# A graph layer with routed experts: three parts instead of two, two rows of a chunk normalized on GpSimd, and other numbers in the table that sets the order

## The chip, the cores and the metric

The kernel runs on one core of one Trainium2 chip. The metric is device time in microseconds for one execution. Three runs of the kernel before took 1494.88, 1497.17 and 1503.07 us, so the median is 1497.17 us. The profiled execution is a fourth one; it took 1489.54 us.

## The reference, cut to what matters

There are 6250 nodes with 256 features and 106250 edges sorted by destination. All numbers are float32.

```
xn = layernorm(x)
agg = segment_sum(xn[src] * edge_weight, dst);  gnn = agg @ weight
q, k, v = split(xn @ Wqkv.T) in 8 heads of 64;  k, v normalized per head
mix = (q @ (k^T v) / n) @ Wout.T + bout          # k^T v sums over all nodes
x2 = x + gnn + mix
y = layernorm(x2)
top 2 of 16 experts by y @ gate_w + gate_b, softmax over the two
moe = sum over the two of (relu(y @ w1[e] + b1[e]) @ w2[e] + b2[e])
out = x2 + layernorm(y + moe) * gamma + beta
```

## The kernel before

**Rows and batches.** The nodes are 49 row tiles of 128. The edges are 70 batches of up to 12 gathers; one gather (GpSimd, line 873) fetches 128 normalized rows from DRAM by source. There are 831 gathers. TensorE sums a batch with 12 small products (line 1528, called edges below), places the sum in its window of nodes (line 1537), and VectorE adds it (line 1132). The ring of gathered rows holds two batches, so the gathers of batch b wait until the edges of batch b-2 are done (`after(pool, batch_done, b - 1)` ahead of line 873).

**Opening.** The rows of x come in 7 chunks of 7 tiles. VectorE takes statistics (line 1020), ScalarE the root (line 885), VectorE the reciprocal (line 1029); then ScalarE normalizes 5 tiles of the chunk (line 889) and VectorE 2 (line 1035). SyncE writes each chunk to the table in DRAM (line 713). The first gather waits for the whole table and for a flag (line 1081) that says the edge tables have the expected form.

**Work beside the gathers.** On TensorE, between the edges of one batch and the next, stand: `kv` of each row tile (keys, values and their sum), one `mid` (the weights folded together), `mix` of a group of two row tiles (attention and graph output), `gate` of a group (VectorE and ScalarE: normalize, choose two experts), `rank`, `slots`, `line`, `list` of a stretch of row tiles (places of its rows in lists by expert; only rank and list have products on TensorE, lines 1637 and 1645; slots is some 9 us of small VectorE instructions, lines 1283 to 1356). GpSimd then scatters the stretch's rows to their slots (line 843, two per row tile), and expert tiles of 128 slots can run (`moe`: a transposition at line 1652, first layer 1664, second layer 1677, and the sum with the bias on VectorE, line 1461).

**Parts.** `PT` cuts the 49 row tiles into parts. An expert's rows fill tiles of 128 slots, and within a part a tile is shared by stretches; at the end of a part each expert's last tile is closed, however full. `SUB` cuts the parts into stretches. The reference's own routing, counted with the inputs of the run, gives 89 tiles in part 0 (row tiles 0 to 39) and 28 in part 1 (40 to 48). When all tiles of a part are done, GpSimd picks up its results (line 856, two per row tile) and VectorE finishes the rows (`fin1`, `fin2`, lines 1479 to 1509) and SyncE stores them. Picks use the ring, so they start only after the last batch.

**The order.** `plan()` walks the batches with a table of prices in us (`EDGES_PE`, `KV_PE`, `TAKEN_PE` for an expert tile, `LANDS` and others) and writes down which pieces stand after the edges of which batch, and where in GpSimd's stream scatters and picks stand. Every engine follows that list in order; nothing is chosen at run time but whether a possible tile exists. What stands after the last batch is the tail.

Of the kernel before, what the change touches and what calls it, by code (L numbers as in the profile page):

```python
# [8 lines left out]
ALU = mybir.AluOpType  # L9
# [7 lines left out]
CH = 7  # L17
NC = 7
NT = NC * CH
# [19 lines left out]
NW = NP // GW  # L39
ACT_ROWS = 5  # L40

E, F = 16, 512
# [9 lines left out]

PT = (0, 40, NT)
SUB = (0, 8, 16, 24, 32, 36, 40, NT)
NPART, NSUB = len(PT) - 1, len(SUB) - 1
# [79 lines left out]
GATHER, SCATTER = 1.254, 1.28  # L135
EDGES_PE, KV_PE, MID_PE, MIX_PE, GATE_PE, TAKEN_PE, LEFT_PE = 2.4, 5.0, 18.0, 2.3, 0.01, 3.9, 0.5
RANK_PE, LAG, SPARE, LANDS = 0.7, 6.0, 4.0, 4.0

# [219 lines left out]
def gps_layer(nc, x, src, dst, first_dst, edge_w, gnn_w, wkv, wq, wout, bout, gate_w, gate_b,  # L358
# [5 lines left out]
    with ExitStack() as ctx:  # L364
# [3 lines left out]
        def sem(name):  # L368
            return ctx.enter_context(nc.semaphore(name))
# [4 lines left out]
        X2 = sb("X2", [P, NT, D])  # L374
# [151 lines left out]
        dve_consts = sem("dve_consts")  # L526
        tables_in = sem("tables_in")
        later_in = sem("later_in")
        x_in = sems("x_in", NC + 1)
# [3 lines left out]
        normed = sem("normed")  # L533
        dve_normed = sem("dve_normed")
        table_out = sem("table_out")
# [144 lines left out]
        TABLES = [(dstrel[:, :].bitcast(I32), dst), (first_i, first_dst.to_broadcast([P, NG]))]  # L680
        CONSTS = [(ew[:, :], edge_w), (src_sb[:, :], src), (wkv_sb, wkv)]
        LATER = [(wq_sb, wq), (wout_sb, wout), (gnn_sb[:, :, 0:D], gnn_w), (gate_sb[:, :, :], gate_w),
# [10 lines left out]
        def rows_of(t, q, n=1):  # L693
            return t[q * P:(q + n) * P, :].rearrange("(j p) d -> p j d", p=P)
# [6 lines left out]
        def _(sp):  # L701
# [8 lines left out]
            for c in range(NC):  # L710
                sp.wait_ge(normed, ACT_ROWS * (c + 1))
                sp.wait_ge(dve_normed, c + 1)
                sp.dma_start(rows_of(table, c * CH, CH), X2[:, c * CH:(c + 1) * CH, :]).then_inc(table_out, 16)
            for o, i in LATER:
                sp.dma_start(o, i).then_inc(later_in, 16)
# [79 lines left out]
        def _(pool):  # L795
# [18 lines left out]
            for s, t in dealt.items():  # L814
# [4 lines left out]
                          allow_small_or_imprecise_dtypes=True).then_inc(pool_consts, 1)  # L819

            pool.wait_ge(table_out, 16 * NC)
            pool.wait_ge(flag_ready, 1)
# [58 lines left out]
        def _(act):  # L881
            act.wait_ge(pool_consts, 2)
            for c in range(NC):
                act.wait_ge(stats_done, c + 1)
                act.activation(std0[:, c * CH:(c + 1) * CH], mv[:, c * CH:(c + 1) * CH, 1], ACT.Sqrt,
                               bias=eps_t[:]).then_inc(std_done, 1)
                act.wait_ge(rstd_done, c + 1)
                for q in range(c * CH, c * CH + ACT_ROWS):
                    act.activation(X2[:, q, :], X2[:, q, :], ACT.Identity, bias=nmr[:, q:q + 1],
                                   scale=rstd[:, q:q + 1]).then_inc(normed, 1)  # L890
# [122 lines left out]
        def _(dve):  # L1013
# [12 lines left out]
            def scale_chunk(c):  # L1026
# [6 lines left out]
                dve.drain().then_inc(rstd_done, 1)  # L1033
                for q in range(c * CH + ACT_ROWS, (c + 1) * CH):
                    ins = dve.tensor_scalar(X2[:, q, :], X2[:, q, :], rstd[:, q:q + 1], nmr[:, q:q + 1],
                                            ALU.mult, ALU.add)
                ins.then_inc(dve_normed, 1)
            stats_chunk(0)
# [44 lines left out]

            dve.wait_ge(consts_in, 16 * len(CONSTS))
            k3 = wkv_sb.rearrange("p k (h d) -> p (k h) d", d=DH)
# [434 lines left out]
        def _(pe):  # L1520
# [183 lines left out]
            pe.wait_ge(normed, ACT_ROWS * NC)  # L1704
            pe.wait_ge(dve_normed, NC)
            pe.wait_ge(flag_ready, 1)
# [72 lines left out]
```

## Time and profile before

| | us |
|---|---|
| median of three runs | 1497.17 |
| profiled execution, its own time | 1489.54 |
| its span, first to last instruction | 1487.7 |
| TensorE busy | 1023.5 |
| GpSimd busy | 1007.7 |
| first gather starts | 53.4 |
| edges of the last batch start | 1260.3 |
| first expert tile of part 1 starts | 1323.1 |
| last expert tile ends on TensorE | 1450.2 |

The span has three stretches: the opening up to the first gather, 1207 us in which GpSimd gathers and scatters while the other engines work between batches, and a tail of 227 us. Two engines are busy for two thirds of the span each, so the shares alone don't say what bounds it: the waits of each stretch do. A row's start is counted from the span's start.

### The profile page before, as it was taken

Reading aid. Unit: us, or ns where it says so; the run is one execution under the profiler, and the core shown is the slowest. Engines: PE = TensorE matmul, PEld = TensorE weight load, DVE = VectorE, ACT = ScalarE, POOL = GpSimd, SP = SyncE. Lnnn points to the kernel's source line nnn. Section 1 sums busy time; section 2 is a strip of 40 time slices with the busy share of each in tenths; the row PEclk is TensorE's granted clock in tenths of the full one; section 3 lists DMA queues with packets and bytes.
Section 4 is the critical chain, followed back from the end, with each engine's and each line's share of the span. In section 5 each row is a group of like instructions: output and inputs, shape, how many; then the busy total and the mean of one; then the engine's idle time right before and its main releaser. Section 6 shows DMA issues by size and latency. Waiting matters only on the chain. (4 is left out here: it accounts for less than half of the span.)

```text
span 1487.7 us, 21903 instructions
## 1 busy us (share of the span) xinstructions
PE 1023.5 (69%) x6498; PEld 761.3 (51%) x6498; DVE 651.1 (44%) x2406; ACT 406.0 (27%) x1085; POOL 1007.7 (68%) x1094
## 2 busy tenths in 40 slices
PE   0099999997764889744199641896674997558880
PEld 0055555554542778522077520775553886447870
DVE  7545454443457422323223332225144233528776
ACT  4144343332121324201033210332221332214330
POOL 4477777777755767777777777777767774176734
PEclk9999999999977899956589865999886999889995
DMA  9676656733321998633489534895855985289883
GB/s 336 173 239 206 205 163 196 235 105 104 99 81 68 318 358 279 214 105 103 160 268 362 179 103 138 279 329 194 301 206 189 329 303 188 82 296 346 268 300 117
DMA packets 153597, 317.09 MB, mean 213 GB/s; under 512 B 24608, under 2 KB 97568, under 8 KB 153344
## 3 DMA queue, kind: packets, MB, share of 16 engines
q0 software_dynamic: 49296, 134.68, 28.9%
q1 hardware_dynamic: 64320, 142.25, 27.3%
q10 hardware_dynamic: 39856, 38.67, 7.7%
q8 instruction: 56, 0.92, 0.3%
q14 instruction: 69, 0.57, 0.1%
HBM read 251.15 MB, written 64.36 MB: 212 GB/s over the span
## 5 line engine op out<-in xcount | busy, mean ns | idle before, releaser
L873 POOL DMA_INDIRECT ring<-normed_rows,src_sb x831 | 799.4, 962 | 326.0 <-issue 286.5
L1528 PE MATMUL ps<-ring,S 128*32 128x256 f32 x1680 | 133.8, 462 | 233.0 <-DMA ring<-normed_rows,src_sb 148.2
L1664 PE MATMUL ps<-room 128*128 128x128 f32 x1872 | 240.1, 284 | 17.8 <-DMA room<-in_w1b 17.0
L1664 PEld LDWEIGHTS ps<-room 128*128 128x128 f32 x1872 | 228.4, 199 | 22.9 <-issue 20.6
L1677 PE MATMUL ps<-room 128*128 128x256 f32 x936 | 225.4, 384 | 9.2 <-issue 9.2
L1528 PEld LDWEIGHTS ps<-ring,S 128*32 128x32 f32 x1680 | 58.8, 126 | 281.4 <-issue 252.6
L1461 DVE TENSOR_TENSOR desk<-ps,room 128x256 f32<-128x256 f32 x121 | 51.2, 424 | 330.6 <-PE ps L1677 324.7
L1677 PEld LDWEIGHTS ps<-room 128*128 128x128 f32 x936 | 171.6, 194 | 30.9 <-issue 12.0
L1555 PE MATMUL ps<-room,tT 128*128 128x512 f32 x392 | 177.4, 595 | 0.0
L983 ACT ACTIVATE room<-ps,room 128x128 f32<-128x128 f32 x468 | 133.4, 368 | 122.7 <-PE ps L1664 122.7
L843 POOL DMA_INDIRECT rows_by_slot<-X,slot_i x98 | 96.1, 981 | 78.9 <-DVEq L1353 47.8
L856 POOL DMA_INDIRECT ring<-results_by_slot,slot_i x98 | 96.8, 988 | 65.8 <-issue 49.0
L1008 ACT COPY accs<-ps 128x256 f32<-128x256 f32 x70 | 26.1, 372 | 412.9 <-PE ps L1528 412.9
L1149 DVE TENSOR_REDUCE kv_var<-room 128x16 f32<-128x1024 f32 x49 | 59.8, 1220 | 128.8 <-ACT room L917 128.8
L1555 PEld LDWEIGHTS ps<-room,tT 128*128 128x128 f32 x392 | 71.3, 192 | 70.8 <-issue 70.8
L962 ACT COPY room<-ps 128x256 f32<-128x256 f32 x121 | 44.6, 369 | 173.3 <-PE ps L1652 97.7
L917 ACT ACTIVATE room<-ps 128x1024 f32<-128x1024 f32 x49 | 50.1, 1023 | 119.8 <-PE ps L1555 119.8
L1652 PE MATMUL ps<-ident,room 128*128 128x128 f32 x242 | 50.1, 290 | 34.0 <-DMA room<-rows_by_slot 26.4
L1625 PE MATMUL ps<-M,tT 128*128 128x288 f32 x196 | 68.5, 481 | 1.3 <-ACT tT L897 1.3
L1180 DVE SCALAR_TENSOR_TENSOR X<-X,std,bout_b 128x256 f32<-128x256 f32 x49 | 23.0, 483 | 105.3 <-PE ps L1545 105.3
L1563 PEld LDWEIGHTS ps<-room 128*128 128x128 f32 x392 | 52.4, 195 | 23.5 <-issue 20.7
L1545 PE MATMUL ps<-ident,X 128*128 128x128 f32 x196 | 45.2, 316 | 25.9 <-ACT tT L897 25.4
(226 smaller groups left out, 1176.5 us busy)
## 6 DMA issues: line engine op xcount, KB each, us to landing
room<-in_w2b SPq DMA_DIRECT2D x87, 640.0 KB, 6.6
room<-in_w1b SPq DMA_DIRECT2D x87, 514.0 KB, 5.7
room<-rows_by_slot SPq DMA_DIRECT2D x121, 128.0 KB
results_by_slot<-desk ACTq DMA_DIRECT2D x121, 128.0 KB
rows_by_slot<-desk ACTq DMA_DIRECT2D x6, 2432.0 KB
ring<-normed_rows,src_sb POOLq DMA_INDIRECT x831
normed_rows<-X SPq DMA_DIRECT2D x7, 896.0 KB, 7.7
result<-ring SPq DMA_DIRECT2D x49, 128.0 KB, 4.0
```

Of the source, the lines that this page charges most:

```text
L843: pool.indirect_dma_start(out=xs[p], out_offset=bass.IndirectOffsetOnAxis(ap=slot_i[:, k, q:q + 1], axis=0), in_=X2[:, q, :], in_offset=No ...
L856: pool.indirect_dma_start(out=pk[i][k][:, n, :], out_offset=None, in_=ys[p], in_offset=bass.IndirectOffsetOnAxis(ap=slot_i[:, k, q:q + 1], ...
L873: pool.indirect_dma_start(out=ring[:, b % 2 * BT + m, :], out_offset=None, in_=table, in_offset=bass.IndirectOffsetOnAxis(ap=src_sb[:, b * ...
L983: last = act.activation(hT[g % 2][:, f, :], hps[g % 2][:, f * TS:(f + 1) * TS], ACT.Relu, bias=w1_sb[g % WB][:, KD * F + f:KD * F + f + 1])
L1149: dve.tensor_reduce(kv_var[q % 2][:, :], sq.rearrange("p (h d) -> p h d", d=DH), AX.X, ALU.add).then_inc(kv_var_done, 1)
L1461: dve.tensor_tensor(yo[g % 2], ops, w2_sb[g % WB][:, W2ROW:], ALU.add).then_inc(y_done, 1)
L1528: mm = pe.matmul(acc[w * W:(w + 1) * W, :], S[b % 2][:, m, :], ring[:, b % 2 * BT + m, :], start=(t == 0), stop=(t == GT - 1), skip_group_ ...
L1555: mm = pe.matmul(wide[q % 2][:, h * 512:(h + 1) * 512], tT[n % 2][:, k * P:(k + 1) * P], wkv_sb[:, k, h * 512:(h + 1) * 512], start=(k == ...
L1563: mm = pe.matmul(dotps[:, a, :], vs[q % 2][:, a * P:(a + 1) * P], ks[q % 2][:, a * P:(a + 1) * P], start=(q == 0 and a == 0), stop=False, ...
L1625: pe.matmul(lps_wide[n % 2], tT[t % 2][:, k * P:(k + 1) * P], M[:, k, :], start=(k == 0), stop=False, skip_group_check=True)
L1664: mm = pe.matmul(hps[g % 2][:, f * TS:(f + 1) * TS], w1_sb[g % WB][:, k * F + f * P:k * F + (f + 1) * P], xgT[g % 2][:, k, :], start=(k == ...
L1677: mm = pe.matmul(ops, hT[g % 2][:, f, :], w2_sb[g % WB][:, f * D:(f + 1) * D], start=(f == 0), stop=(f == FC - 1))
```

## The change

`PT` becomes (0, 38, 43, 49) and `SUB` (0, 8, 16, 24, 32, 38, 43, 49). By the same count of the reference's routing the three parts have 86, 21 and 23 tiles, 130 in place of 117. GpSimd normalizes the two tiles of a chunk that VectorE did. ScalarE takes the root of chunk c+1 ahead of normalizing chunk c. Edge weights and the key and value weights are loaded after the table is written, in place of before. Seven prices of the table are raised; `plan()` then spreads `kv` over 21 batches in place of 19, puts the expert tiles at one to three a batch where there were two to four, and leaves 47 taken tiles after the edges and pieces of the last batch (31 before).

```
-PT = (0, 40, NT)
-SUB = (0, 8, 16, 24, 32, 36, 40, NT)
+PT = (0, 38, 43, NT)
+SUB = (0, 8, 16, 24, 32, 38, 43, NT)
-EDGES_PE, KV_PE, MID_PE, MIX_PE, GATE_PE, TAKEN_PE, LEFT_PE = 2.4, 5.0, 18.0, 2.3, 0.01, 3.9, 0.5
-RANK_PE, LAG, SPARE, LANDS = 0.7, 6.0, 4.0, 4.0
+EDGES_PE, KV_PE, MID_PE, MIX_PE, GATE_PE, TAKEN_PE, LEFT_PE = 2.9, 5.2, 18.0, 2.5, 0.01, 4.6, 0.5
+RANK_PE, LAG, SPARE, LANDS = 1.2, 6.0, 4.0, 6.0
...
-        CONSTS = [(ew[:, :], edge_w), (src_sb[:, :], src), (wkv_sb, wkv)]
+        CONSTS = [(src_sb[:, :], src)]
+        EDGE_CONSTS = [(ew[:, :], edge_w), (wkv_sb, wkv)]
...
                 sp.wait_ge(normed, ACT_ROWS * (c + 1))
-                sp.wait_ge(dve_normed, c + 1)
+                sp.wait_ge(pool_normed, POOL_ROWS * (c + 1))
                 sp.dma_start(rows_of(table, c * CH, CH), X2[:, c * CH:(c + 1) * CH, :]).then_inc(table_out, 16)
+            for o, i in EDGE_CONSTS:
+                sp.dma_start(o, i).then_inc(edge_consts_in, 16)
...
+            for c in range(NC):
+                pool.wait_ge(rstd_done, c + 1)
+                for q in range(c * CH + ACT_ROWS, (c + 1) * CH):
+                    pool.tensor_scalar(X2[:, q, :], X2[:, q, :], rstd[:, q:q + 1], nmr[:, q:q + 1],
+                                       ALU.mult, ALU.add).then_inc(pool_normed, 1)
...
-            for c in range(NC):
+
+            def root_chunk(c):
                 act.wait_ge(stats_done, c + 1)
                 act.activation(std0[:, c * CH:(c + 1) * CH], mv[:, c * CH:(c + 1) * CH, 1], ACT.Sqrt,
                                bias=eps_t[:]).then_inc(std_done, 1)
+            root_chunk(0)
+            for c in range(NC):
+                if c + 1 < NC:
+                    root_chunk(c + 1)
                 act.wait_ge(rstd_done, c + 1)
...
-                for q in range(c * CH + ACT_ROWS, (c + 1) * CH):
-                    ins = dve.tensor_scalar(X2[:, q, :], X2[:, q, :], rstd[:, q:q + 1], nmr[:, q:q + 1],
-                                            ALU.mult, ALU.add)
-                ins.then_inc(dve_normed, 1)
...
-            dve.wait_ge(consts_in, 16 * len(CONSTS))
+            dve.wait_ge(edge_consts_in, 16 * len(EDGE_CONSTS))
```

ScalarE's stream in the opening of the kernel before is a root (std) and five rows (X) for each chunk in turn.

```order
L885 ACTIVATE std<-mv,eps_t 128x7
L889 ACTIVATE X<-X,nmr,rstd 128x256 x5
L885 ACTIVATE std<-mv,eps_t 128x7
L889 ACTIVATE X<-X,nmr,rstd 128x256 x5
L885 ACTIVATE std<-mv,eps_t 128x7
L889 ACTIVATE X<-X,nmr,rstd 128x256 x5
L1008 COPY accs<-ps 128x256
```

ScalarE's stream at the end of the opening of the changed kernel, up to the same copy of batch 0's sum.

```order
L897 ACTIVATE std<-mv,eps_t 128x7
L905 ACTIVATE X<-X,nmr,rstd 128x256 x5
L897 ACTIVATE std<-mv,eps_t 128x7
L905 ACTIVATE X<-X,nmr,rstd 128x256 x5
L897 ACTIVATE std<-mv,eps_t 128x7
L905 ACTIVATE X<-X,nmr,rstd 128x256 x10
L1024 COPY accs<-ps 128x256
```

The root of the last chunk now stands ahead of the last ten rows, where it stood ahead of the last five.

TensorE's stream of the kernel before at the first `rank` (the two products of desk), which is the last piece after the edges (ring,S) of batch 22; the pairs of M and gnn_sb are the two row tiles of a `mix`.

```order
L1545 MATMUL ps<-ident,X 128x128 x4
L1625 MATMUL ps<-M,tT 128x288 x2
L1628 MATMUL ps<-gnn_sb,aggT 128x272 x2
L1625 MATMUL ps<-M,tT 128x288 x2
L1628 MATMUL ps<-gnn_sb,aggT 128x272 x2
L1637 MATMUL ps<-desk,upper 128x128
L1637 MATMUL ps<-desk,ones 128x128
L1528 MATMUL ps<-ring,S 32x256 x12
L1537 MATMUL ps<-Pm,accs 128x128 x2
L1528 MATMUL ps<-ring,S 32x256 x12
```

The same place of the changed kernel, after the edges of batch 24.

```order
L1649 MATMUL ps<-desk,upper 128x128
L1649 MATMUL ps<-desk,ones 128x128
L1557 MATMUL ps<-ident,X 128x128 x4
L1637 MATMUL ps<-M,tT 128x288 x2
L1640 MATMUL ps<-gnn_sb,aggT 128x272 x2
L1637 MATMUL ps<-M,tT 128x288 x2
L1640 MATMUL ps<-gnn_sb,aggT 128x272 x2
L1540 MATMUL ps<-ring,S 32x256 x12
L1549 MATMUL ps<-Pm,accs 128x128 x2
L1540 MATMUL ps<-ring,S 32x256 x12
```

Between the rank and the next edges now stand `slots` and `gate` of other engines and a `mix`, where the edges of the next batch followed at once.

GpSimd's stream of the kernel before from its first gather on: gathers (ring<-normed_rows), scatters (rows_by_slot) and at the end picks (ring<-results_by_slot); the first scatter stands behind 303 gathers.

```order
L873 DMA ring<-normed_rows,src_sb 128x256 x85
L843 DMA rows_by_slot<-X,slot_i 12672x256 x8
L873 DMA ring<-normed_rows,src_sb 128x256 x60
L843 DMA rows_by_slot<-X,slot_i 12672x256 x8
L873 DMA ring<-normed_rows,src_sb 128x256 x89
L843 DMA rows_by_slot<-X,slot_i 4736x256 x18
L856 DMA ring<-results_by_slot,slot_i 128x256 x98
```

The end of GpSimd's stream in the changed kernel.

```order
L884 DMA ring<-normed_rows,src_sb 128x256 x111
L854 DMA rows_by_slot<-X,slot_i 12160x256 x12
L884 DMA ring<-normed_rows,src_sb 128x256 x97
L854 DMA rows_by_slot<-X,slot_i 3712x256 x10
L884 DMA ring<-normed_rows,src_sb 128x256 x26
L854 DMA rows_by_slot<-X,slot_i 3968x256 x12
L867 DMA ring<-results_by_slot,slot_i 128x256 x98
```

Ahead of the last gather stand 86 scatters in place of 80, and behind it 12 in place of 18.

## Rows read from the trace of the kernel before

**Rows 1.** The page's costliest groups: count, then busy us, mean ns, idle before.

```profile
L873 POOL DMA_INDIRECT ring<-normed_rows,src_sb x831 | 799.4, 962 | 326.0 <-issue 286.5
...
L1664 PE MATMUL ps<-room 128*128 128x128 f32 x1872 | 240.1, 284 | 17.8 <-DMA room<-in_w1b 17.0
...
L843 POOL DMA_INDIRECT rows_by_slot<-X,slot_i x98 | 96.1, 981 | 78.9 <-DVEq L1353 47.8
```

**Rows 2.** Waits of GpSimd: us in total, times, longest.

```profile
POOL ring L873 <- PE ps L1528: 39.5, 14, 15.1
```

**Rows 3.** Busy time by stretch: engines, clock, DMA share, GB/s.

```profile
0.00:54.00 54.00, 0.56 (x2) 0.50 (x2) 39.47 (x151) 20.69 (x43) 15.91 (x68) 1.00 0.98 316
...
1323.00:1450.00 127.00, 113.19 (x730) 100.83 (x730) 92.32 (x275) 46.68 (x161) 74.46 (x75) 0.97 0.92 313
```

**Rows 4.** Timeline of the opening: start, us, instruction, idle before and releaser.

```profile
11.48 0.52 POOL L799 MEMSET room<- 128x512 f32 x1
...
37.01 0.73 DVE L1035 TENSOR_SCALAR X<-X,rstd,nmr 128x256 f32<-128x256 f32 x2
...
39.74 0.20 DVE L1029 RECIPROCAL rstd<-std 128x7 f32<-128x7 f32 x1 [2.00 <-ACT std L885]
...
40.25 2.57 ACT L889 ACTIVATE X<-X,nmr,rstd 128x256 f32<-128x256 f32 x5 [0.54 <-DVEq L1033]
...
51.37 0.14 DVE L1081 CAST flag<-ps 1x1 int32<-1x1 f32 x1 [0.74 <-PE ps L1702]
...
53.40 1.14 POOL L873 DMA_INDIRECT ring<-normed_rows,src_sb  x1 [37.42 <-issue]
```

**Rows 5.** Timeline of TensorE from the batch of mid to the second rank.

```profile
360.45 2.79 PE L1528 MATMUL ps<-ring,S 128*32 128x256 f32 x24 [4.58 <-issue]
...
388.79 1.50 PE L1528 MATMUL ps<-ring,S 128*32 128x256 f32 x24
...
438.75 0.38 PE L1545 MATMUL ps<-ident,X 128*128 128x128 f32 x2
443.54 0.44 PE L1545 MATMUL ps<-ident,X 128*128 128x128 f32 x2 [4.41 <-ACT tT L897]
...
452.75 0.49 PE L1637 MATMUL ps<-desk,upper 128*128 128x128 f32 x2 [3.30 <-DVE desk L1272]
...
466.62 2.79 PE L1528 MATMUL ps<-ring,S 128*32 128x256 f32 x24 [10.52 <-DVE aggT L1132]
...
485.85 0.80 PE L1637 MATMUL ps<-desk,upper 128*128 128x128 f32 x2 [8.05 <-DVE desk L1272]
```

**Rows 6.** Timeline of VectorE, the end of the first slots.

```profile
461.12 0.18 DVE L1350 CAST slot_i<-slot_f 128x16 int32<-128x16 f32 x1
```

**Rows 7.** Timeline of GpSimd, the last gather.

```profile
1247.84 0.95 POOL L873 DMA_INDIRECT ring<-normed_rows,src_sb  x1 [0.30 <-issue]
```

**Rows 8.** Timeline of TensorE in the tail.

```profile
1260.32 1.50 PE L1528 MATMUL ps<-ring,S 128*32 128x256 f32 x24
...
1282.74 0.85 PE L1637 MATMUL ps<-desk,upper 128*128 128x144 f32 x2 [8.04 <-DVE desk L1272]
...
1323.09 0.66 PE L1652 MATMUL ps<-ident,room 128*128 128x128 f32 x2 [13.62 <-DMA room<-rows_by_slot]
...
1333.48 0.38 PE L1652 MATMUL ps<-ident,room 128*128 128x128 f32 x2
...
1337.21 0.38 PE L1652 MATMUL ps<-ident,room 128*128 128x128 f32 x2
...
1448.21 1.97 PE L1677 MATMUL ps<-room 128*128 128x256 f32 x8 [0.56 <-issue]
```

**Rows 9.** DMA issues of expert weights and table: count, KB each, us to landing.

```profile
room<-in_w2b SPq DMA_DIRECT2D x87, 640.0 KB, 6.6
room<-in_w1b SPq DMA_DIRECT2D x87, 514.0 KB, 5.7
...
normed_rows<-X SPq DMA_DIRECT2D x7, 896.0 KB, 7.7
```

More of the change, by code:

```diff
@@ L40 @@
 ACT_ROWS = 5
+POOL_ROWS = CH - ACT_ROWS
 E, F = 16, 512
@@ L527, in gps_layer @@
         tables_in = sem("tables_in")
+        edge_consts_in = sem("edge_consts_in")
         later_in = sem("later_in")
@@ L533, in gps_layer @@
         normed = sem("normed")
-        dve_normed = sem("dve_normed")
+        pool_normed = sem("pool_normed")
         table_out = sem("table_out")
@@ L1704, in _ @@
             pe.wait_ge(normed, ACT_ROWS * NC)
-            pe.wait_ge(dve_normed, NC)
+            pe.wait_ge(pool_normed, POOL_ROWS * NC)
             pe.wait_ge(flag_ready, 1)
```

## Prediction

> **What bounds the kernel now.** I read the groups of the page first, then the waits, then the timeline of each stretch. A gather costs GpSimd 0.96 us and 0.30 us of issue ((286.5 - 37.4) / 830), a scatter 0.98 and 0.30 [rows 1, 4]; so 831 gathers and the 80 scatters ahead of the last gather with a few slower ones, are some 1150 us of the 1195 between the first gather at 53.4 and the last one's end at 1248.8 [rows 7]. The rest, 44.5 us, are waits, 39.5 of them for the edges of two batches before [rows 2]. From the first gather to the last the kernel is therefore bound by GpSimd's stream, plus what TensorE makes it wait. Behind the last batch TensorE bounds it: rank at 1282.7, a wait of 13.6 us for scattered rows, then 28 tiles from 1323.1 to 1450.2 (1448.21 + 1.97), which is 4.54 us a tile, where a tile that waits for nothing takes 3.73 (1333.48 to 1337.21), and 37.5 us of picks and last rows [rows 8]. So four things count: when the first gather starts, how long GpSimd waits, how many scatters stand ahead of the last gather, and how many tiles stand in the tail.
>
> **The change part by part.**
>
> Opening. VectorE loses 7 x 0.65 us (two rows take 0.73, overlapping at the ends) and its wait of 2.00 us for the last root, which no longer stands behind five rows of ScalarE [rows 4]. The last reciprocal is thus done 6.55 us earlier, at 33.65 in place of 40.2. The work on the edge tables that follows took 10.5 us (40.2 and 0.75 for two rows, to the flag at 51.5), and ends at 44.2. ScalarE then has ten rows left, 5.1 us from 33.2: 38.4 in place of 42.8. A piece of the table takes 7.7 us to land [rows 9], so the table is there at 46. With the same 1.9 us from the later of flag and table to the gather, the first gather starts at 48.0, 5.4 us earlier. GpSimd's price for a row of 256 is not in the trace; the nearest row is its fill of 512 elements, 0.52 us, so 0.26, and from above five times that, 1.3. Two rows at 1.3 are hidden by VectorE's 3.7 us a chunk. 1.5 MB (edge weights and key weights) move from ahead of the table's writes to beside the first gathers. The DMA engines were 0.98 busy at 316 GB/s in this stretch [rows 3], so they cost between 0 and 4.7 us there. I take 0.4, nearest to nothing, as batch 0's edges wait for gathers that end at 67. **Opening: -5 us** (bounds -7 and 0).
>
> First lists. `kv` takes two batches more and never makes GpSimd wait, before or after. At 264 gathers of 1.26 us, batch 21's end at 384, and its edges start at 386. `mid` and a mix cost 28.3 us (360.45 to 388.79) [rows 5], so batch 22's edges stand at 414. A gate ahead of a mix costs 10.7 us, 438.75 to the idle start 449.45, of which 4.4 are TensorE's wait for ScalarE, which normalizes the gate's rows before it copies the mix's; a mix alone is some 5.5. Edges are 1.5. Then batch 23's edges stand at 414 + 1.5 + 5.5 + 10.7 = 432, batch 24's at 432 + 1.5 + 21.4 = 455. After batch 24 come two such pairs (21.4), edges 1.5, rank 4.0 (3.30 of waiting and the products [rows 5]), and then, new, slots, gate and a mix: slots took 8.6 us from the rank at 452.75 to the cast's end at 461.3 [rows 6], the gate and ScalarE's rows about 4.5, the mix 5: together 45, so batch 25's edges stand at 500. Before, the edges of batch 23 followed the rank at once, and slots ran beside them. Behind the new mix are queued all later pieces of TensorE, and for its edges GpSimd waits. Batch 26's edges follow about 10 us later (before 13.2, 453.40 to 466.62), batch 27's 37 after that: rank came 20 us after such edges (466.62 to 485.85), and slots, gate, line and list behind it are 17.
>
> GpSimd against that: batch 24's gathers wait 1.5 us, batch 25's 2.4, batch 26's (ready at 448.5, edges of 24 done at 456) 7.8, and batch 27's, ready at 471.4, until the edges of 25 are done at 501: 30 us, where the longest wait before was 15.1 [rows 2]. Scatter 1 waits 2.6 for its slots; nine tiles after batch 27 cost 1.3; later batches, with three tiles in place of four, some 2.5. Sum 48 against 44.5. **First lists and later waits: +3.5 us.** The bounds are wide, -36 (all as laid out, 12 us of waits) and +20.
>
> Scatters. Rows 40 to 42 are scattered ahead of the last gather now: 6 x 1.28 = **+7.7 us**. The last gather then ends at 1248.8 - 5 + 3.5 + 7.7 = 1255, and the last edges start 11.5 later, as before.
>
> Tail. By the count of the reference's routing the new parts have 86, 21 and 23 tiles, and the order puts 3 real ones of part 0, 21 and 23 in the tail (before 3 and 28; 1872 products of 16 a tile are the 117 tiles [rows 1]). Let T be the start of the last edges. Before, the end was T + 227.4. Now: to the end of rank T + 25 (before 23.5; one more tile, one row less of mix). A tile's y sum waits on VectorE for slots, 8.6 us against the tile's 3.73, so 5 more: T + 30. Three tiles at 4.54: T + 43.6. While these run the last stretch is routed, and its 12 scatters end by T + 52, so the wait of 13.6 us goes; the 21 tiles of the middle part stand in its place, and are longer. 44 tiles at 4.54 are 200 us: T + 243.6. From below they are 44 x 3.73 = 164, from above the transfers: 31 weight loads of 1.18 MB (15 and 16 experts, [rows 9]), 86 picks, 43 stores and 88 tile rows of 0.131 MB are 65 MB, 208 us at the 313 GB/s that the tail had at a share of 0.92 [rows 3]. I take 200, the value of the same kind of tiles beside the same picks. Six picks fewer at the end: 37.5 - 7.5 = 30. End T + 273.6. **Tail: +46 us** (bounds +8 and +65).
>
> The Trainium skill's page "DMA: Bandwidth & Descriptors", section Specifications, gives about 358 GB/s of HBM for one core; the estimate from that page for the 65 MB is 182 us, so by it transfers would not bind the tail's tiles, and by the row they would, by 8 us. No row of a whole stretch here is above 316.
>
> Sum: 1487.7 - 5 + 3.5 + 7.7 + 46 = 1540 of span, 1542 with the 1.84 us around it. The median of the runs shown is 7.6 us above the profiled execution; with that I predict **1549 us**.
>
> **The rivals.**
>
> The order does as laid out (chance 0.19). If gate and mix cost TensorE little once slots is under way, GpSimd waits 12 us, not 48. For it: the two gates of the tail together made TensorE wait only 8.0 us [rows 8]. Against it: VectorE and ScalarE follow the same list in order, and the 4.4 us at a gate are in the trace [rows 5]. 1549 - 36 = 1513, still slower.
>
> Transfers bind the middle part (0.14). Its 21 tiles get 15 loads and nearly all of part 0's picks and stores: 38 MB, 122 us at 313 GB/s, against 95 at 4.54. For it: a share of 0.92 already. Against it: picks can slip beside the last 23 tiles, which have fewer of them. 1576. By the 358 GB/s of the Trainium skill's page "DMA: Bandwidth & Descriptors", Specifications, these 38 MB would be an estimated 107 us.
>
> TensorE runs the tail without a gap (0.13); this is the one on the faster side. With the middle part's tiles ready before the last routing, rows and weights are always there, so 47 tiles take 3.73 in place of 4.54, 38 us less, and the 30 us before the first of them shrink by up to 10. Alone it gives 1501, and it decides for faster when GpSimd's waits also stay under some 40 us: at 30 the time is 1483. For it: a granted clock of 0.97 in the tail [rows 3] and the two tiles that follow each other without a gap [rows 8]. Against it: 15 to 16 experts in 21 to 23 tiles ask for a new weight at 0.7 of the tiles, where it was 16 in 28.
>
> GpSimd's rows are slow (0.05): at over 1.85 us a row, two of them exceed VectorE's 3.7 us a chunk and the table waits for GpSimd. At 2.6 the first gather starts near 58, +10 on the forecast, 1559. The change then doesn't do what it says.
>
> **How the numbers follow.** The forecast itself has 0.49, with 1530 to 1568 of its own. What a measurement here can tell from no change is about 0.5%, so 1490 to 1505. Slower by more: the forecast, the transfers, slow GpSimd rows, 0.15 of the first rival and 0.01 of the third: 0.84. The gapless tail gives the rest of its chance as faster 0.08 and same 0.04, the first rival's low end 0.02 and 0.02. Range 1500 to 1578.
>
> **What would show it.** In the profile of the changed kernel the first gather should start at 46 to 50; GpSimd's longest wait for edges should stand at batch 27 and be 20 to 35 us; its waits for edges in total 40 to 55; the last edges should start at 1255 to 1275; behind them 47 tiles with no wait for scattered rows over 5 us; and the tail should be 265 to 285 us. The prediction is wrong if the last gather ends before 1230, or if the tail is under 250: then the tiles of the middle part ran at nearly 3.73, or were in part run before the last batch.

## The result and the profile after

The changed kernel takes 1565.1 us (median of 4 runs, 1561.1 to 1567.1), the kernel before 1498.6 in the same comparison: a ratio of 1.0439, 95% interval 1.0402 to 1.0476. The profiled execution took 1561.1 us and spans 1559.3, against 1487.7 before. So 71.6 us were added, and nearly all of them lie behind the last batch.

GpSimd's side of the trace of the changed kernel, its timeline first (start, us, instruction, idle before), then its waits for TensorE's edges (total, times, longest):

```profile
30.18 1.09 POOL L829 TENSOR_SCALAR X<-X,rstd,nmr 128x256 f32<-128x256 f32 x2 [2.62 <-DVEq L1049]
33.90 2.81 POOL L829 TENSOR_SCALAR X<-X,rstd,nmr 128x256 f32<-128x256 f32 x4 [2.62 <-DVEq L1049]
...
47.59 1.15 POOL L884 DMA_INDIRECT ring<-normed_rows,src_sb  x1 [10.88 <-issue]
...
497.00 1.15 POOL L884 DMA_INDIRECT ring<-normed_rows,src_sb  x1 [28.59 <-PE ps L1540]
...
1247.34 0.95 POOL L884 DMA_INDIRECT ring<-normed_rows,src_sb  x1 [0.30 <-issue]
```

```profile
POOL ring L884 <- PE ps L1540: 40.3, 4, 28.6
```

The first gather starts 5.8 us earlier than in [rows 4]. The wait of 28.6 us is the one ahead of batch 27; the total of the waits is 0.8 us above [rows 2]. Six scatters more stand ahead of the last gather, and still it ends at 1248.3, where it was 1248.8 in [rows 7].

TensorE in the tail, the same points as in [rows 8]:

```profile
1260.55 1.50 PE L1540 MATMUL ps<-ring,S 128*32 128x256 f32 x24
...
1282.98 0.74 PE L1649 MATMUL ps<-desk,upper 128*128 128x96 f32 x2 [6.49 <-DVE desk L1284]
...
1301.55 1.97 PE L1689 MATMUL ps<-room 128*128 128x256 f32 x8 [0.92 <-PEq L653]
1315.14 0.66 PE L1664 MATMUL ps<-ident,room 128*128 128x128 f32 x2 [11.63 <-DMA room<-rows_by_slot]
...
1420.68 1.97 PE L1689 MATMUL ps<-room 128*128 128x256 f32 x8 [0.56 <-issue]
1435.01 0.66 PE L1664 MATMUL ps<-ident,room 128*128 128x128 f32 x2 [12.37 <-DMA room<-rows_by_slot]
...
1529.66 1.96 PE L1689 MATMUL ps<-room 128*128 128x256 f32 x8 [0.56 <-issue]
```

The last edges start where they did. From there the end is 298.7 us away (1559.3 - 1260.6), against 227.4. Between the two stand the middle part's 21 tiles and a second boundary between parts: a wait of 11.6 us ahead of the middle part and one of 12.4 ahead of the last, where one of 13.62 stood before. The page's groups count the tiles of the whole program:

```profile
L1676 PE MATMUL ps<-room 128*128 128x128 f32 x2080 | 265.5, 283 | 18.9 <-DMA room<-in_w1b 13.6
```

2080 products of 16 a tile are 130 tiles where [rows 1] have 117: a third part pads its experts' tiles once more.

What SyncE does at the first boundary, and who it waits for (the timeline, then the waits of 1296 to 1312):

```profile
1294.79 0.34 SPq L736 DMA_DIRECT2D room<-rows_by_slot  x1
1309.49 0.33 SPq L747 DMA_DIRECT2D room<-in_w1b  x1
1310.02 0.41 SPq L749 DMA_DIRECT2D room<-in_w2b  x1
1311.11 1.16 SPq L736 DMA_DIRECT2D room<-rows_by_slot  x2
```

```profile
SPq L747 <- ACTq L659: 9.0, 1, 9.0
```

ScalarE's stores of the last three tiles' results, in its timeline:

```profile
1304.13 4.15 ACTq L984 DMA_DIRECT2D results_by_slot<-desk  x3
```

Line 659 is the leaving out of an optional run, tiles that only longer lists would need. SyncE may load the next part's first weights and rows only when ScalarE has stored the last results of the part before and has then counted the optional visits as done. So the first rows are asked for 7.6 us after the last product (1303.5) and land 4.0 us later. The scatters have nothing to do with it: the middle part's rows were scattered in batch 67. At the second boundary the rows are again asked for 7.6 us after the last product (1422.65), but there something else holds SyncE. It stands with the stores of finished row pairs (line 779), which wait for VectorE's finals (the waits of 1412 to 1432, then the timeline):

```profile
SPq L779 <- DVE ring L1521: 11.3, 2, 5.9
```

```profile
1430.22 1.19 SPq L736 DMA_DIRECT2D room<-rows_by_slot  x2
```

The wait for ScalarE stood in the kernel before too, hidden in its 13.62 us. There SyncE's timeline has the weights 4.3 us after the last product (1323.09 - 13.62), and only then, by its waits of 1309 to 1324, does it wait for the scatters:

```profile
1313.80 0.34 SPq L742 DMA_DIRECT2D room<-in_w1b  x1
1314.33 0.33 SPq L744 DMA_DIRECT2D room<-in_w2b  x1
1320.92 1.16 SPq L731 DMA_DIRECT2D room<-rows_by_slot  x2
```

```profile
SPq L634 <- DMA rows_by_slot<-X,slot_i: 5.7, 1, 5.7
SPq L742 <- ACTq L657: 4.6, 1, 4.6
```

### The profile page after: what moved, and what is told of

It reads as the page before. It is cut to its first block and busy times, and to the rows that moved or that the text cites. A ratio compares the mean times of both kernels' runs of the same rounds, so it can differ in the third digit from the quotient of the medians.

```text
span 1559.3 us, 23013 instructions
## 1 busy us (share of the span) xinstructions
PE 1082.4 (69%) x6834; PEld 812.1 (52%) x6834; DVE 651.8 (42%) x2411; ACT 425.1 (27%) x1149; POOL 1013.8 (65%) x1110
## 5 line engine op out<-in xcount | busy, mean ns | idle before, releaser
L1676 PE MATMUL ps<-room 128*128 128x128 f32 x2080 | 265.5, 283 | 18.9 <-DMA room<-in_w1b 13.6
L1676 PEld LDWEIGHTS ps<-room 128*128 128x128 f32 x2080 | 253.0, 199 | 23.5 <-issue 17.1
L1689 PE MATMUL ps<-room 128*128 128x256 f32 x1040 | 248.7, 382 | 10.7 <-issue 9.8
L1473 DVE TENSOR_TENSOR desk<-ps,room 128x256 f32<-128x256 f32 x133 | 56.2, 424 | 364.9 <-PE ps L1689 361.1
L1689 PEld LDWEIGHTS ps<-room 128*128 128x128 f32 x1040 | 188.9, 192 | 34.7 <-issue 14.3
L999 ACT ACTIVATE room<-ps,room 128x128 f32<-128x128 f32 x520 | 148.2, 368 | 138.2 <-PE ps L1676 137.9
L1567 PE MATMUL ps<-room,tT 128*128 128x512 f32 x392 | 181.3, 606 | 0.0
L978 ACT COPY room<-ps 128x256 f32<-128x256 f32 x133 | 48.9, 368 | 203.5 <-PE ps L1664 106.5
L1664 PE MATMUL ps<-ident,room 128*128 128x128 f32 x266 | 54.3, 287 | 50.2 <-DMA room<-rows_by_slot 36.3
L1664 PEld LDWEIGHTS ps<-ident,room 128*128 128x128 f32 x266 | 34.6, 145 | 69.0 <-issue 41.7
```

Source lines behind the costliest of these rows:

```text
L999: last = act.activation(hT[g % 2][:, f, :], hps[g % 2][:, f * TS:(f + 1) * TS], ACT.Relu, bias=w1_sb[g % WB][:, KD * F + f:KD * F + f + 1])
L1473: dve.tensor_tensor(yo[g % 2], ops, w2_sb[g % WB][:, W2ROW:], ALU.add).then_inc(y_done, 1)
L1567: mm = pe.matmul(wide[q % 2][:, h * 512:(h + 1) * 512], tT[n % 2][:, k * P:(k + 1) * P], wkv_sb[:, k, h * 512:(h + 1) * 512], start=(k == ...
L1664: mm = pe.transpose(xgps[:, k * TS:(k + 1) * TS], xg[g % XB][:, k * P:(k + 1) * P], ident[:])
L1676: mm = pe.matmul(hps[g % 2][:, f * TS:(f + 1) * TS], w1_sb[g % WB][:, k * F + f * P:k * F + (f + 1) * P], xgT[g % 2][:, k, :], start=(k == ...
L1689: mm = pe.matmul(ops, hT[g % 2][:, f, :], w2_sb[g % WB][:, f * D:(f + 1) * D], start=(f == 0), stop=(f == FC - 1))
```

## Experiments

Ratios are to the kernel before, run on the same chip. "Tail" is from the start of the last edges to the end of the span. The first three kernels take the change apart.

**Opening alone.** Parts and prices of before, everything else as changed (the diffs are against the changed kernel where nothing else is said).

```diff
-PT = (0, 38, 43, NT)
-SUB = (0, 8, 16, 24, 32, 38, 43, NT)
+PT = (0, 40, NT)
+SUB = (0, 8, 16, 24, 32, 36, 40, NT)
-... TAKEN_PE, LEFT_PE = 2.9, 5.2, 18.0, 2.5, 0.01, 4.6, 0.5
-RANK_PE, LAG, SPARE, LANDS = 1.2, 6.0, 4.0, 6.0
+... TAKEN_PE, LEFT_PE = 2.4, 5.0, 18.0, 2.3, 0.01, 3.9, 0.5
+RANK_PE, LAG, SPARE, LANDS = 0.7, 6.0, 4.0, 4.0
```

> The kernel before with the new opening alone (GpSimd normalizes two rows of a chunk, the roots run one chunk ahead, edge weights and K/V weights load behind the table); parts and prices as before. Theory A, the opening's gain of 5.8 us passes through the whole row of gathers, because the front is bound by GpSimd's issue of gathers: last gather ends near 1243, last edges near 1254.5, tail unchanged at 227: 1492 to 1494 against 1498.5. Theory B, later waits of GpSimd for edges take it back, as in the changed kernel, whose last gather ended within 0.5 us of before: 1497 to 1500, waits for edges grown from 44.5 to about 50 us.

Measured 1488.4 against 1494.1: 0.9959 (0.9934 to 0.9985), 5.7 us less. First gather 47.78, last gather's end 1239.7, waits for edges 37.9 in 14. Theory A holds in the median: what the opening gives passes through the row of gathers. In the profiled execution the last edges start 9.2 us earlier (1251.1) and the tail is 5.2 longer (232.6 for 227.4), though its order is that of before; a difference of some 5 us between two single executions is therefore no finding by itself.

**Opening and prices, two parts.** Only PT and SUB go back.

> The changed kernel with the parts of before (cut at row tile 40, stretches 32 to 36 to 40), so opening and new prices stay. Theory A, the prices alone push tiles out of the front: 37 real tiles behind the last edges where before has 31, six more at 4.5 us, less some 2 us of the wait for scattered rows, which they hide: tail 252 us, front as in the changed kernel (last edges 1260): about 1516. Theory B, the third part is what costs and the prices are harmless: tail 227 to 232, about 1494 to 1499.

Measured 1513.8: 1.0131 (1.0077 to 1.0185); tail 254. Theory A: the prices alone, with nothing else of the order changed by hand, cost 0.0172 over the opening, 26 us, by six tiles more in the tail (39 counted in the trace where the opening alone has 33).

**Opening and three parts, old prices.** Only the two price lines go back.

> The changed kernel with the prices of before, so opening and three parts stay. Theory A: nine fewer tiles behind the last edges than in the changed kernel (38 of 47), at 4.5 us each, both boundary waits stay: tail 298.7 - 40 = 258 us; front 1255 to 1260 as the shorter waits allow: about 1517 to 1522. Theory B, the third part itself costs all of the loss, whatever the prices: 1555 to 1565. Theory C, the prices are all of the loss: 1494 to 1499.

Measured 1546.4: 1.0348 (1.0293 to 1.0403); tail 284.5. Neither number was right; B's share is nearer. Six tiles fewer than in the changed kernel were left for the tail (44 of 50 counted), not nine. Both boundary waits stay (12.0 and 12.4 us), and the first now stands at 1272, since the first part is done before the last routing. Over the opening the third part costs 0.0389, 58 us. That 13 more tiles at 4.54 would be 59 is a coincidence: between the two profiles, 11 tiles more stand behind the last edges, the boundary waits are 10.5 us more, the tail is 51.9 longer, and the last edges start 6.3 later. Prices and parts together cost 72, not 84: they push out some of the same tiles.

The other kernels ask what the two boundary waits are.

**Loads across the boundary.** The optional run between two parts is not there (these inputs never take it), and SyncE goes on loading.

```diff
+if first < n and SUB[s + 1] < NT:
+    n = first
 ...
-if j == 0:
+if j == 0 and r not in NEXT.values():
 ...
 load_rows(r, j + 3)
+if r in NEXT and j + 3 >= n:
+    if j + 3 == n:
+        t = RUNS[NEXT[r]][0]
+        sp.wait_ge(listed, LISTS[t])
+        sp.wait_ge(scattered[t], 32 * (SUB[t + 1] - SUB[t]))
+    load_rows(NEXT[r], j + 3 - n)
 load_weights(r, j + 2)
+if r in NEXT and j + 2 >= n:
+    load_weights(NEXT[r], j + 2 - n)
```

> The changed kernel with two things gone at the ends of its first and second part: the branch for a part with more tiles than usual, which these inputs leave out, and the break in SyncE's loads, which now go on into the next part's first three tiles and two weight sets from the last three tiles of the part before. Theory A, the waits of 11.6 and 12.4 us at the two boundaries are this break (the first loads of a part are issued only behind the last results of the part before): they fall to 3 to 5 us each, tail 298.7 to about 283, about 1549 (1545 to 1553). Theory B, transfers bind there (busy share 0.90 beside the middle part) and what is loaded sooner only comes as late: waits move elsewhere, 1559 to 1565.

Measured 1566.8: 1.0467 (1.0411 to 1.0524). The waits shrank to 7.5 and 4.3 us, nearly as theory A had it, and nothing was gained: the tail is 299.1. The time is near theory B's. What is left of the first wait is for ScalarE, whose copy of the next rows stands behind its stores of the last results (TensorE's and ScalarE's timelines); VectorE in turn waited 4.6 us for an earlier store to land before it could write the last of them:

```profile
1318.49 0.66 PE L1675 MATMUL ps<-ident,room 128*128 128x128 f32 x2 [7.53 <-ACT room L989]
```

```profile
1317.97 0.37 ACT L989 COPY room<-ps 128x256 f32<-128x256 f32 x1 [10.50 <-DVE desk L1484]
```

The waits of VectorE from 1311 to 1460 show where the rest went, first in the changed kernel, then in this one:

```profile
DVE desk L1473 <- PE ps L1689: 43.3, 9, 17.4
DVE f_r L1515 <- ACT f_r L1018: 2.8, 4, 1.4
...
DVE desk L1473 <- DMA results_by_slot<-desk: 0.3, 1, 0.3
```

```profile
DVE desk L1484 <- PE ps L1700: 25.1, 7, 8.9
DVE ring L1502 <- DMA ring<-results_by_slot,slot_i: 10.8, 2, 6.3
DVE desk L1484 <- DMA results_by_slot<-desk: 10.1, 4, 4.6
```

VectorE waited for TensorE before; now it waits 10.8 us for picked results and 10.1 for stores of tile results. The tiles start earlier, but the finals of the first part, which the order puts between them, stand on VectorE and wait for their picks, and the next tile's result stands behind them. The wait moved by one engine. Whether the picks and stores were late because they were issued late or because transfers were slow, these rows do not say.

**Fewer bytes by picks.** For theory T, transfers. Each pick of the first part fetches 2 rows in place of 128, so the outputs of these rows are not computed.

```diff
+h = 2 if p == 0 else P
 pool.indirect_dma_start(
-    out=pk[i][k][:, n, :], ... ap=slot_i[:, k, q:q + 1] ...
+    out=pk[i][k][0:h, n, :], ... ap=slot_i[0:h, k, q:q + 1] ...
```

> The changed kernel, whose 76 gathers of results for the first part's 38 row tiles fetch 2 rows each instead of 128 (the output of these tiles is not computed; instructions, order and stores stay): 10 MB less of some 38 MB that move from the first row tile of the middle part (1315) to the first of the last (1435). Theory T, transfers set that stretch of 120 us: it falls by 20 to 30 us, to what 21 tiles at the last part's 4.2 us and one boundary wait need, tail 298.7 to about 270 to 278, 1537 to 1545 where the changed kernel has 1565. Theory D, the break in the loads at a boundary sets it and transfers only colour the tiles' pace: at most 21 x (5.12 - 4.54) = 12 us, both waits stay 11 to 13 us: 1553 or more. Theory O, SyncE's queue in program order, which holds a weight load behind a store that waits for VectorE, sets the pace: under 5 us.

Measured 1559.6: 1.0419 (1.0384 to 1.0454).

**Fewer bytes by weights.** The weight loads of the middle and last part fill half of the partitions; the other half keeps old weights.

```diff
-sp.dma_start(w1_sb[s], w1b[bass.ds(e, 1)] ...
+h = P // 2 if SUB_PART[RUNS[r][0]] else P
+sp.dma_start(w1_sb[s][0:h, :], w1b[bass.ds(e, 1), 0:h] ...
 (w2 the same)
```

> The changed kernel, whose weight loads of the middle and last part fill 64 of 128 partitions (the other half of the weights is stale; instructions and order stay): some 17 loads of 1.18 MB a part are halved, 10 MB less beside the middle part. Theory T: the stretch from 1315 to 1435 falls by 20 to 30 us and the last part by a few more, tail to about 265 to 275, 1530 to 1542 where the changed kernel has 1565. Theory D: at most 12 us, both boundary waits stay. Theory O: under 5 us.

Measured 1562.2: 1.0458 (1.0422 to 1.0495). Busy time from the middle part's first rows to the last part's (columns: length, PE, PEld, DVE, ACT, POOL, granted clock, DMA share, GB/s), in the changed kernel, with thin picks, and with half weights:

```profile
1315.14:1435.01 119.87, 87.48 (x548) 76.03 (x549) 88.37 (x264) 36.33 (x125) 77.48 (x79) 0.93 0.92 321
```

```profile
1324.16:1436.97 112.81, 87.06 (x548) 77.09 (x549) 88.08 (x264) 36.10 (x125) 68.92 (x78) 0.92 0.79 253
```

```profile
1317.62:1437.16 119.54, 88.03 (x549) 77.24 (x549) 88.31 (x264) 36.34 (x125) 76.52 (x79) 0.91 0.90 245
```

A quarter of the bytes is gone in both. In this stretch thin picks save 7 us and half weights nothing, where theory T wanted 20 to 30; over the whole tail the two are alike (294.2 and 294.9 for 298.7), and neither time is clear of the changed kernel's. The Trainium skill's page "Perfetto Trace Analysis", section Identifying the Most-Contended Engine, has the rule: judge DMA by the rate against the peak, since 16 engines make occupancy misleading. With half weights the rate fell from 321 to 245 GB/s, the share only from 0.92 to 0.90, and the stretch kept its length, which agrees with the rule. But it does not clear the transfers, because the engines' time did not fall with the bytes. Packets, MB and share of the engines' time by queue (q1 SyncE's, q0 GpSimd's) in the stretch, in the changed kernel and with half weights:

```profile
q1 hardware_dynamic: 12418, 25.17, 58.3%
q0 software_dynamic: 3741, 10.23, 25.9%
```

```profile
q1 hardware_dynamic: 10427, 16.11, 49.9%
q0 software_dynamic: 3706, 10.13, 31.2%
```

SyncE's bytes fell by 36% and their time only by 14%, and the picks' packets took longer for the same bytes. So half weights hardly relieved the DMA engines, and says little of theory T. Thin picks did relieve them (share 0.79), and bought about a third of what T wanted.

**Both: half weights and loads across.**

> Both edits: the loads go on across the boundaries and the weight loads of the middle and last part are halved (stale other half). Theory T with D behind it: where bytes no longer bind, the break costs what it was thought to cost, so this is 10 to 16 us below the kernel with halved loads alone. If it is within 4 us of that one, the break was never a cost, bytes or not.

Measured 1549.1: 1.0376 (1.0334 to 1.0419), 0.0082 or 12 us below half weights alone. The profiled tails show 6.2 of them (294.9 to 288.7); the rest is the front of two executions. The number expected came: neither half weights nor the mended break moves the end alone, and both together do. Seen from the loads across, half weights take 0.0091 or 14 us off (tail 299.1 to 288.7), and VectorE's wait for stores falls from 10.1 us to this:

```profile
DVE desk L1485 <- DMA results_by_slot<-desk: 2.2, 1, 2.2
```

So transfers are one of the links once the break is mended.

**Thin finals.** VectorE's work on the first part's finals cut to 32 of 256 columns; the rest of these rows is not computed.

```diff
+def wide_of(f):
+    return 32 if PART[FIN[f][0]] == 0 else D
-q, z = a + n, zt[i][:, n, :]
+q, z = a + n, zt[i][:, n, 0:wide_of(f)]
 (and so in each of the five operations)
```

> The changed kernel, whose final sums and normalizations of the first part's 38 row tiles (19 pairs, woven between the tiles of the middle part) are computed on 32 of 256 columns (the rest of these outputs is not computed; every instruction, wait and transfer stays): VectorE's 4.7 us of work for a pair falls to some 2. Theory F, the engines' order paces the middle part: a tile's result waits on VectorE behind a pair's final, the next W2 load waits on SyncE for that result, and the next W1 load stands behind it: 21 tiles fall from 5.12 to about 4.2 us (-19) and the second boundary wait by 2 to 4 us, tail 298 to 274 to 280, 1542 to 1548 where the changed kernel has 1565. Theory O, SyncE's order and the latency of its loads alone: under 6 us. Theory T, transfers, which halved weights and left-out gathers have already spoken against: under 3 us.

Measured 1562.6: 1.0434 (1.0375 to 1.0492). Theory F fell, as far as VectorE's arithmetic goes; the order of its work is as before. VectorE is busy 46.5 us of the stretch instead of 88.4, and the stretch goes from 119.9 to 117.6; VectorE just waits longer for TensorE (76.1 us where it was 43.3).

**SyncE in another order.** A visit is a place in the order for an expert tile; W1 and W2 are the weights of its two layers. The W2 load of a visit comes one visit later, and a pair's store two pairs after its final in place of one.

```diff
-load_weights(r, j + 2)
+load_weights(r, j + 2, 0)
+load_weights(r, j + 1, 1)
 ...
-for o in late:
-    store(o)
-late.clear()
+if len(late) > 1:
+    store(late.pop(0))
 late.append(f)
```

> The changed kernel with SyncE's queue in another order: the W2 load of a visit is issued one visit later than its W1 load, so that it no longer waits for a result of VectorE with the next W1 and row loads behind it, and a pair's store two pairs later than its final instead of one. All is computed. Theory O: the waits of SyncE for VectorE in the middle stretch, 28.6 us for results and 14.0 us for finals, are what W1 loads come late by (PE waits 7.9 us for W1 there): the middle part falls by 8 to 15 us, tail 298 to 283 to 290. Theory F, VectorE's own order sets the pace: under 5 us.

Measured 1551.7: 1.0371 (1.0316 to 1.0426), 10 us under the changed kernel, 6.5 of them in the profiled tail (292.2). The two intervals overlap; the next kernel, with the same order in it and the loads across, has one that lies clear of the changed kernel's. SyncE's waits from 1310 to 1430, in the changed kernel and in this one:

```profile
SPq L749 <- DVE desk L1473: 28.6, 11, 5.2
SPq L779 <- DVE ring L1521: 14.0, 5, 5.9
```

```profile
SPq L748 <- ACTq L659: 11.7, 2, 9.0
...
SPq L748 <- DVE desk L1472: 5.5, 3, 3.0
...
SPq L779 <- DVE ring L1520: 1.6, 5, 0.5
```

Theory O holds: the time fell by 10 us, within its 8 to 15, while the profiled stretch (7.3) and tail stay just outside its numbers. Of 42.6 us of waiting for VectorE 7.1 are left, TensorE's waits for W1 fall from 7.9 us to 1.9 (1318 to 1420), and the stretch to 112.6:

```profile
1319.66:1432.25 112.59, 86.88 (x548) 77.38 (x549) 88.63 (x264) 36.02 (x125) 73.75 (x76) 0.92 0.96 335
```

Both boundary waits stay (12.9 and 11.3), with the leaving-out as SyncE's longest wait. The edit moves two things, W2 loads and stores; no run separates them.

**SyncE in the other order, and loads across.** The two diffs together.

> The changed kernel with SyncE's queue in the other order (W2 load a visit later, stores two pairs later) and the loads going on across the two part boundaries (the branch for longer lists, which these inputs leave out, is not there). What is open: why the loads across the boundaries alone gained nothing (1.0467 of before) while the other order alone gained 10 us (1.0371). Theory O+D: the two are in series. A load that starts earlier across a boundary was used up by the next W1 loads, which stood behind SyncE's waits for VectorE; with these gone, the boundary waits of 12.9 and 11.3 us fall to 3 to 5 each and stay gained: 12 to 18 us under the other order alone, ratio to before 1.025 to 1.029, tail 290.7 to 273 to 279. Rival: the loads' own rate (busy share 0.99 in this stretch of the kernel with the other order) is the floor now: within 5 us of the other order alone, 1.034 to 1.040.

Measured 1551.6: 1.0371 (1.0349 to 1.0394), the same as the order alone. The rival's number came, and theory O+D fell. The rival's cause, the rate, does not fit as given (share 0.93, 327 GB/s, under the 0.96 and 335 above). VectorE again waits for picks and stores, late or slow:

```profile
DVE ring L1503 <- DMA ring<-results_by_slot,slot_i: 14.6, 5, 6.7
DVE desk L1485 <- PE ps L1701: 14.6, 5, 8.5
DVE desk L1485 <- DMA results_by_slot<-desk: 10.4, 3, 5.0
```

One of them, in VectorE's timeline:

```profile
1328.65 0.88 DVE L1503 SCALAR_TENSOR_TENSOR ring<-ring,prob,X 128x256 f32<-128x256 f32 x2 [6.66 <-DMA ring<-results_by_slot,slot_i]
...
1331.13 0.42 DVE L1485 TENSOR_TENSOR desk<-ps,room 128x256 f32<-128x256 f32 x1
```

A tile's result at 1331.13 stands behind a pair's final that waited 6.7 us for its picks, and TensorE's next second layer, which needs the result's bank, stands 4.4 us until 1331.65.

**A cut at 41.** With the opening and the old prices, the two parts cut one row tile later (the diff is against the opening alone); and the same with SyncE's other order.

```diff
-PT = (0, 40, NT)
-SUB = (0, 8, 16, 24, 32, 36, 40, NT)
+PT = (0, 41, NT)
+SUB = (0, 8, 16, 24, 32, 38, 41, NT)
```

> The new opening with two parts and the old prices, the cut moved from row tile 40 to 41 (stretches 32 to 38 to 41 to 49), so that the last part has 27 visits where 29 were, 16 scatters where 18 were, and the first part one tile more behind the last edges, beside the wait for scattered rows of 13.9 us. Theory: two tiles less at 4.9 us behind that wait, which starts 2.5 us earlier on the scatters' side or 2 us later on the tiles' side: 6 to 10 us under the kernel with the opening alone, ratio to before 0.988 to 0.992. Rival: the loads of the last part's first rows come only behind the first part's last results, the wait keeps its end, and picks and weights share the transfers as before: within 3 us of the opening alone (0.994 to 0.998).

Measured 1487.3: 0.9936 (0.9912 to 0.9960). It lies between the two expectations, and its interval overlaps that of the opening alone: the cut is not shown to give anything. The wait ahead of the last part is now 9.3 us. It ends 63.2 us after the start of the last edges, where the opening alone has 62.9: it keeps its end, as the rival had it.

> The kernel with the new opening, old prices and the cut at row tile 41, with SyncE's queue in the same other order. All is computed. Theory O: 25 tiles behind the last scatter at 4.9 us fall to about 4.5: 8 to 12 us under the kernel without the new queue order, ratio to before 0.985 to 0.989. Theory F: within 4 us of it, 0.991 to 0.996.

Measured 1470.8: 0.9829 (0.9789 to 0.9869), 16 us below the same cut without the queue's order, more than theory O's bounds. In the profiles 9.1 us of this are in the tail (228.4 to 219.3); the last gather also ends earlier, at 1238.1 for 1248.4, about where the opening alone had it. GpSimd waited 30.1 us for edges in that execution, 42.3 in the other. That the queue's order did this is not shown: in the changed kernel it left the front as it was (42.1 us for 40.3). The last part's stretch, first without and then with it:

```profile
1322.55:1455.53 132.98, 113.97 (x702) 101.92 (x702) 87.88 (x260) 45.25 (x154) 77.43 (x79) 0.91 0.89 299
```

```profile
1319.63:1437.93 118.30, 107.49 (x702) 97.41 (x702) 87.94 (x260) 44.50 (x154) 77.06 (x78) 0.97 0.95 330
```

The same 702 products take 14.7 us less. This kernel computes everything, and it is faster than the kernel before and the changed one.

## Why the prediction came out as it did

The sign and most of the size were right for the reason given: the order leaves 47 tiles behind the last batch, and the front gives nothing back to pay for them. 1565 lies in the range and 16 us above the 1549. Two errors of opposite sign make most of this up: the last edges started 6 us earlier than forecast, and the tail came out 25.1 longer. The rest is that the median lay 4.0 us above the profiled execution, not 7.6.

*Opening, -5.* Right. First gather at 47.59 for a forecast 48.0. GpSimd's row cost 0.55 us (1.09 for two; only the last two rows took longer, so that the last four came to 2.81), between the fill's 0.26 and the bound of 1.3, and the moved 1.5 MB did not show: the DMA engines run at 328 GB/s in the first 48 us, against 316 in [rows 3]. The opening alone is worth 5.7 us, and the fourth rival, slow rows, is out.

*First lists and later waits, +3.5.* The place was right, the longest wait at batch 27 with 28.6 us for a forecast 30; edges of batch 25 at 495 for 500. The rest of the waits was overrated: 40.3 us in all, not 48 (the 44.5 before included some that are not waits for edges, so the like-for-like change is +0.8). The first rival, in which the order does as laid out and the waits are 12 us, is out.

*Scatters, +7.7.* The six are there, and yet the last gather ended 0.5 us earlier than before: -5.8 + 0.8 + 7.7 would be 2.7 later. The missing 3 us are a wait of the scatters for VectorE, 2.9 us before the last gather in the kernel before and gone now; GpSimd's other differences between the first gather and the last nearly cancel.

*Tail, +46.* This term was mis-sized, at +71, and the step is the sentence that the wait of 13.6 us goes because the middle part's 21 tiles stand in its place. Its other pieces were near: the first part's last product ends at T + 43.0 for T + 43.6, the 44 tiles take 107.5 + 96.6 = 204 us for 200, the end 27.7 for 30. The 200 is in part luck: at 4.54 a tile the middle part was to take 95 us and the last 104. What was not in the sum are the 11.6 and 12.4 us ahead of the middle and the last part, and these 24 us are nearly the whole excess. I had put the 13.6 us of [rows 8] down to the scatters, since the releaser named was the load of scattered rows. That load stood behind two things on SyncE: ScalarE's leaving-out (4.6 us of wait) and then the scatters (5.7). With the scatters long done, the first remains, and grows to 9.0 at the first boundary; at the second, SyncE's stores behind VectorE's finals take its place. The first chain was in the trace of before, in SyncE's own waits, and the prediction did not follow it.

That SyncE's break makes about half of the two waits is shown (24.0 us became 11.8 without it); that mending it alone saves time is refuted. Across the boundary the loads came sooner, and VectorE then waited for picks and stores. The middle part is a ring of engines that each work in the order of one list, and several of its links are nearly equally late: the break, the weight loads behind SyncE's waits for VectorE, and the transfers of picks, stores and weights. Another queue order alone took out 10 us; the break alone, half weights alone and VectorE's arithmetic gave nothing that is clear, and fewer picks 7 us of the stretch in one execution. What the floor of that stretch is below 112.6 us stays open: TensorE's products fill some 87 of it, the DMA engines are busy for 0.96 of it, and no run laid the finals later behind their picks.

Of the points that were to show it, the first four came (first gather, longest wait, total of the waits, last edges), and the last two failed together: two waits for rows over 5 us, and a tail of 298.7 for 265 to 285.

*The rivals.* Transfers binding the middle part gave 122 us for its tiles, and my 4.54 a tile gave 95; they took 107.5, or 119.9 with the wait behind them. Neither is right. The rival's price, 313 GB/s as a ceiling, is refuted by 30 us in the kernel with loads across that moved 383 (last column). That transfers alone set the stretch is refuted too: thin picks took the share to 0.79 and saved 7 us, and another queue order saved as much with every byte moved. That they are one of the links is not refuted, as half weights with the loads across show.

```profile
1405.00:1435.00 30.00, 19.94 (x121) 16.44 (x119) 23.09 (x70) 8.44 (x30) 16.16 (x16) 1.00 1.03 383
```

The 358 GB/s of the Trainium skill's page "DMA: Bandwidth & Descriptors", section Specifications, was the better guide there, and this window lies above it too. A gapless tail (third rival) has no support: tiles took 5.1 us in the middle part and 4.2 in the last.

## What to carry to other kernels

When a wait is to be covered by other work, follow the instruction that ends it back along its own queue and list everything it stands behind; the releaser that a profile names is only the last of them. A further part costs its padding and its boundary, whatever it hides (13 tiles and one more boundary here, 58 us in all). And a queue that issues loads in program order should not hold a load whose buffer is freed late ahead of one whose buffer is free: another order of loads and stores was worth 10 to 16 us here, where the new opening gave 5.7. And bytes left out of a transfer count only if the time of its packets falls with them.

## What was not expected of the hardware

With weight loads into half of the partitions, SyncE's queue moved 36% fewer bytes in only 14% less of the DMA engines' time (25.17 MB at 58.3%, 16.11 at 49.9%), so the share stayed at 0.90 while the rate fell from 321 to 245 GB/s. GpSimd normalizes a row of 256 in 0.55 us (two in 1.09), where VectorE took 0.73 for two [rows 4]. And TensorE's granted clock was 0.97 in the stretch of 1319.63 to 1437.93 that has no long wait, 0.91 in the one of the same products with waits of 3 us between them, and the same products were busy 107.5 us there instead of 114.0.
